# One layer of a diffusion transformer on one core: order inside the norm periods, the queue of the weights' loads, and where operands stand in SBUF

## The reference

```python
attn_in = _adaln(x, cond, ln1_w, ln1_b, g1_w, g1_b, b1_w, b1_b)
x = _attn(attn_in, attn_in, sa_wq, sa_wkv, sa_wo, sa_bo) + x
cross_in = _adaln(x, cond, ln1_w, ln1_b, g1_w, g1_b, b1_w, b1_b)
ctx_n = _ln(context, ca_lnc_w, ca_lnc_b)
x = _attn(cross_in, ctx_n, ca_wq, ca_wkv, ca_wo, ca_bo) + x
ffn_in = _adaln(x, cond, ln2_w, ln2_b, g2_w, g2_b, b2_w, b2_b)
h = gelu(ffn_in @ ff_w1 + ff_b1)
x = h @ ff_w2 + ff_b2 + x
# _attn: softmax(rope(q) @ rope(k).T / 8) @ v, then @ wo + bo
```

## The kernel before

| operand | before | with the change |
|---|---|---|
| xn_hi, xn_lo, ctx_hi, ctx_lo | 128 | 128 |
| w_hi, w_lo: weights of q and k | 192 | 192 |
| w_hi, w_lo: weights of v and of the output | 192 | 64 |
| o_hi, o_lo | 0 | 128 |
| hi (q, k) | 192, 0 | 0, 0 |
| lo (q, k) | 192, 0 | 192, 192 |
| pick, max_rows | 64, 192 | 192, 192 |
| hid_hi and hid_lo, w1, w2 | 0, 192, 192 | 0, 192, 192 |

## Time and profile before

### The profile page before, as it was taken

One profiled execution on the slowest core, in us unless ns is written; L12 is line 12 of the kernel. 1 busy time (PEld: TensorE's weight loads), 2 busy tenths in 40 slices (PEclk: granted clock), 3 DMA queues, 4 the chain that ended last, 5 costly groups with the idle time before them and its releaser, 6 DMA issues.

```text
span 1088.9 us, 18356 instructions
## 1 busy us (share of the span) xinstructions
PE 1071.9 (98%) x6908; PEld 758.4 (70%) x6908; DVE 854.3 (78%) x1017; ACT 640.5 (59%) x912; POOL 775.8 (71%) x502
## 2 busy tenths in 40 slices
PE   8899999999999999999999999999999999999998
PEld 6667766676667666776667766666677766666997
DVE  5887878778787787788888888888888888887555
ACT  6575565665666555566766555665555545786521
POOL 2688767787877876689999966887678767764210
PEclk8999999999999999999999999999999999999999
DMA  5322111311221111211122111221121111300001
GB/s 174 94 69 49 38 38 40 83 40 31 54 64 36 39 41 39 68 31 39 40 50 56 40 34 39 70 50 40 39 67 35 37 40 40 118 1 2 20 20 40
DMA packets 61096, 52.86 MB, mean 49 GB/s; under 512 B 23504, under 2 KB 43984, under 8 KB 60752
## 3 DMA queue, kind: packets, MB, share of 16 engines
q1 hardware_dynamic: 59232, 50.10, 19.4%
q10 hardware_dynamic: 1776, 1.59, 0.5%
HBM read 15.75 MB, written 2.10 MB: 16 GB/s over the span
## 4 chain that ended last, share of the span: by engine, by line
PE 91%; ACT 3%; DVE 2%; DMA 1%; issue 1%; POOL 1%; SPq 0%; ACTq 0%; POOLq 0%
PE ps L1029 18%; PE ps L813 9%; PE ps L814 8%; PE ps L815 8%; PE ps L966 6%; PE ps L888 6%; PE ps L1000 6%; PE ps L1014 6%; PE ps L972 5%; PE ps L970 5%; PE ps L968 5%; PE ps L1125 4%; PE ps L859 1%; PE ps L829 1%; PE ps L901 1%
## 5 line engine op out<-in xcount | busy, mean ns | idle before, releaser
L646 ACT ACTIVATE probs<-ps 128x1024 f32<-128x1024 f32 x256 | 262.4, 1026 | 198.7 <-PE ps L972 177.3
L1227 DVE TENSOR_REDUCE neg_max<-ps 128x2 f32<-128x1024 f32 x256 | 300.7, 1224 | 43.4 <-PE ps L1000 43.3
L503 POOL TENSOR_TENSOR acc<-acc,probs 128x1024 f32<-128x1024 f32 x126 | 301.2, 2391 | 18.1
L1029 PE MATMUL ps<-probs,v 128*64 128x512 f32 x1024 | 230.7, 592 | 0.0
L498 POOL TENSOR_TENSOR acc<-probs 128x1024 f32<-128x1024 f32 x64 | 152.3, 2380 | 43.6 <-ACT probs L646 43.6
L512 POOL TENSOR_TENSOR eo<-tmp 128x512 f32<-128x512 f32 x63 | 89.0, 1412 | 122.4 <-DVE tmp L1254 121.7
L1029 PEld LDWEIGHTS ps<-probs,v 128*64 128x64 f32 x1024 | 73.8, 137 | 145.5 <-issue 145.5
L1254 DVE TENSOR_TENSOR tmp<-ps,rope 128x1024 f32<-128x1024 f32 x126 | 148.4, 1213 | 16.2 <-PE ps L859 12.8
L1000 PE MATMUL ps<-hi 64*128 64x512 f32 x512 | 108.0, 410 | 3.3 <-issue 0.9
L966 PE MATMUL ps<-max_rows,pick 64*128 64x512 f32 x512 | 108.6, 412 | 1.9 <-DMA max_rows<-neg_max 1.5
L813 PE MATMUL ps<-xn_hi,w_hi 128*128 128x512 f32 x256 | 106.4, 416 | 1.4 <-DVE xn_lo L358 1.0
(11 more groups left out here) (134 smaller groups left out, 2184.7 us busy)
## 6 DMA issues: line engine op xcount, KB each, us to landing
lo<-eo SPq DMA_DIRECT2D x126, 256.0 KB, 3.3
w_raw<-pack_dram SPq DMA_DIRECT2D x16, 192.0 KB, 3.9
x<-x_dram SPq DMA_DIRECT2D x4, 512.0 KB, 7.9
w_raw<-pack_dram SPq DMA_DIRECT2D x8, 256.0 KB, 3.8
max_rows<-neg_max SPq DMA_DIRECT2D x128, 2.0 KB, 2.1
w_raw<-w_dram SPq DMA_DIRECT2D x2, 1024.0 KB, 5.4
out<-x SPq DMA_DIRECT2D x8, 256.0 KB, 2.2
ctx_in<-ctx_dram SPq DMA_DIRECT2D x4, 384.0 KB, 3.8
```

The source lines that it names most:

```text
L503: pool.tensor_tensor(acc[:, g % 2, :, :], acc[:, g % 2, :, :], probs[:, i, :, :], ALU.add).then_inc(added, 1)
L646: act.activation(probs[:, i, :, :], score_ps(i), ACT.Exp, scale=SCALE).then_inc(exped, 1)
L1029: mm = pe.matmul(av_ps(g)[DH * h:DH * h + DH, :], v[:, u % 2, kt, c:c + DH], probs[:, kt, h, :], start=(kt == 0), stop=(kt == TT - 1))
L1227: dve.tensor_reduce(neg_max[:, g % 2, :, i], peak_ps(i), AX.X, ALU.max, negate=True).then_inc(maxed, 1)
```

## The change

It has five parts.
- ACT: in the norm periods of the context `high_o(p-1)` stands ahead of `high_qk` and of the split of weights.
- The norm's variance plus epsilon: the addition (L1221, 16 times) goes from DVE to ACT, which does it with a bias of epsilon; the logarithm reads the variance itself. `STATS` and the counts of `ln_guess` follow.
- POOL: the biases of batches 1, 2 and 3 are added in periods 16, 21 and 23 rather than 15, 18 and 21.
- SP: `load_weights` stands between `land_max(p+1)` and `land(p+4)` rather than behind both.
- SBUF: the weights are two blocks with 32 elements between them, so that those of the values and of the output stand 128 bytes further on; q and k of `lo` and `hi` lose their offset to each other; gaps, `ones`, `pick` and `o_hi` move with them (the table above).

```diff
-        lo = asb("lo", [128, 2, 4 * N + 16], F32R)
-        gap("gap_hi", 32, attention_only)
-        hi = asb("hi", [128, 2, 2 * N + 16], F32R)
-        gap("gap_w", 32, attention_only)
-        w_hi = asb("w_hi", [128, 4, 2 * D], F32R)
-        w_lo = asb("w_lo", [128, 4, 2 * D], F32R)
+        lo = asb("lo", [128, 4, 2, N], F32R)
+        gap("gap_hi", 16)
+        hi = asb("hi", [128, 2, 2, N], F32R)
+        gap("gap_w", 48)
+        w_hi = asb("w_hi", [128, 2, 4 * D + 32], F32R)
+        w_lo = asb("w_lo", [128, 2, 4 * D + 32], F32R)
...
+        def w_of(tensor, m):
+            return tensor[:, m // 2, m % 2 * 2 * D:(m % 2 + 1) * 2 * D]
...
-        bias_in.update({13: 0, 15: 1, 18: 2, 21: 3})
+        bias_in.update({13: 0, 16: 1, 21: 2, 23: 3})
...
-        STATS = 2 * TT + 1
+        STATS = 2 * TT
...
             for p in range(PAIRS):
                 if is_pair(p + 1):
                     land_max(p + 1)
+                if p % 8 == 1 and p // 8 < NP - 1:
+                    w = p // 8
+                    sp.wait_ge(w_split, 4 * w + 3)
+                    load_weights(w + 1)
                 if is_job(p + 4):
                     land(p + 4)
...
             def guess_rstd(n):
                 act.wait_ge(ln_step, STATS * (n + 1))
-                act.activation(rstd[:, :], var_eps[:, :], ACT.Ln).then_inc(ln_guess, 1)
-                act.wait_ge(ln_guess, 2 * n + 1)
+                act.activation(var_eps[:, :], mean_var[:, :, 1], ACT.Identity, bias=eps[:, :]).then_inc(ln_guess, 1)
+                act.activation(rstd[:, :], mean_var[:, :, 1], ACT.Ln, bias=eps[:, :]).then_inc(ln_guess, 1)
+                act.wait_ge(ln_guess, 3 * n + 2)
                 act.activation(rstd[:, :], rstd[:, :], ACT.Exp, scale=-0.5).then_inc(ln_guess, 1)
...
+                rows_first = p in rows_in_period and order[rows_in_period[p]][0] == C
+                if rows_first:
+                    high_o(p - 1)
                 if is_pair(p + 2):
                     high_qk(p + 2)
                 if p in split_in:
                     split_weights(*split_in[p])
-                if is_pair(p - 1):
+                if is_pair(p - 1) and not rows_first:
                     high_o(p - 1)
...
-                dve.wait_ge(ln_step, STATS * n + 2 * TT)
-                dve.tensor_scalar(var_eps[:, :], mean_var[:, :, 1], EPS, None, ALU.add).then_inc(ln_step, 1)
```

More of the change, by code:

```diff
@@ L55, in build @@
         ident = sb("ident", [128, 128])
-        zero = sb("zero", [128, 1])
+        eps = sb("eps", [128, 1])
         cols = sb("cols", [128, 8 * KT + FT])
@@ L73, in asb, with gap @@
             return sb(name, shape, dt, attention_only)
-        def gap(name, size, where=stack):
+        def gap(name, size, where=attention_only):
             sb(name, [128, size], F32, where)
@@ L99, in build @@
         max_rows = asb("max_rows", [128, N], F32R)
[L100 removed]
         pick = asb("pick", [128, 128], F32R)
[L102 removed]
+        ones = asb("ones", [128, DH])
+        gap("gap_o", 48)
         o_hi = asb("o_hi", [128, 3, N], F32R)
         o_lo = asb("o_lo", [128, 3, N], F32R)
[L105 removed]
         av = asb("av", [128, N])
@@ L109, in build @@
         attention_only.close()
-        gap("gap_w1", 40)
+        gap("gap_w1", 40, stack)
         w1_hi = sb("w1_hi", [128, KT, FF], F32R)
@@ L117, in build @@
         w2_raw = sb("w2_raw", [128, FT, D])
-        gap("gap_hid", 16)
+        gap("gap_hid", 16, stack)
         hid_hi = sb("hid_hi", [128, 4, N], F32R)
@@ L126, in build @@
         raw_qk = lo.bitcast(F32)
-        def qk(tensor, slot):
-            return tensor[:, :, slot * N:(slot + 1) * N]
+        def w_of(tensor, m):
+            return tensor[:, m // 2, m % 2 * 2 * D:(m % 2 + 1) * 2 * D]
         def tmp_of(j):
@@ L365, in low_weights @@
                     c = slice(kt * D, (kt + 1) * D)
-                    split = eng.tensor_tensor(w_lo[:, m, c].rearrange("p (e a f) -> p e a f", e=2, a=4),
+                    split = eng.tensor_tensor(w_of(w_lo, m)[:, c].rearrange("p (e a f) -> p e a f", e=2, a=4),
                                               w_raw[:, m, c].rearrange("p (a e f) -> p e a f", e=2, a=4),
-                                              w_hi[:, m, c].rearrange("p (e a f) -> p e a f", e=2, a=4),
+                                              w_of(w_hi, m)[:, c].rearrange("p (e a f) -> p e a f", e=2, a=4),
                                               ALU.subtract)
@@ L454, in _ @@
                     load_ctx_ln()
-                if p % 8 == 1 and p // 8 < NP - 1:
-                    w = p // 8
-                    sp.wait_ge(w_split, 4 * w + 3)
-                    load_weights(w + 1)
                 if p % 8 == 3 and p // 8 < NP - 1:
@@ L481, in _ @@
         def _(pool):
+            pool.memset(eps[:, :], EPS).then_inc(const_ready, 1)
             pool.memset(ident[:, :], 0.0).then_inc(const_ready, 1)
-            pool.memset(zero[:, :], 0.0).then_inc(const_ready, 1)
             pool.memset(pick[:, :].bitcast(F32), 1.0).then_inc(const_ready, 1)
@@ L724, in period @@
                         split_ffw(0, c)
+            act.wait_ge(const_ready, 1)
             guess_rstd(0)
@@ L858, in project_rest @@
                         c = slice(256 + e * 128, 256 + (e + 1) * 128)
-                        mm = pe.matmul(job_ps(j, e), w_[half, 1, c], a_[half, b, 1, :], start=False, stop=(n == 2))
+                        mm = pe.matmul(job_ps(j, e), w_of(w_, 1)[half, c], a_[half, b, 1, :], start=False, stop=(n == 2))
                         if n == 2:
@@ L887, in project_v @@
                         for n, (a_, w_) in enumerate(((a_hi, w_hi), (a_hi, w_lo), (a_lo, w_hi))):
-                            mm = pe.matmul(v_ps(u, tt), a_[:, b, kt, cut], w_[:, 2, c],
+                            mm = pe.matmul(v_ps(u, tt), a_[:, b, kt, cut], w_of(w_, 2)[:, c],
                                            start=first and kt == 0 and n == 0, stop=(phase == 0 and kt == KT - 1 and n == 2),
@@ L900, in project_v_rest @@
                             cut = slice((2 * r + t) * 128, (2 * r + t + 1) * 128)
-                            mm = pe.matmul(v_ps(u, 2 * r + t), a_[half, b, 1, cut], w_[half, 2, 256:512],
+                            mm = pe.matmul(v_ps(u, 2 * r + t), a_[half, b, 1, cut], w_of(w_, 2)[half, 256:512],
                                            start=False, stop=(n == 2), skip_group_check=True)
@@ L962, in score @@
                 half = (slice(0, DH), slice(DH, 128))
-                q_hi, k_hi = qk(hi, g % 2)[:, 0, :], qk(hi, g % 2)[:, 1, :]
-                q_lo, k_lo = qk(lo, g % 4)[:, 0, :], qk(lo, g % 4)[:, 1, :]
+                q_hi, k_hi = hi[:, g % 2, 0, :], hi[:, g % 2, 1, :]
+                q_lo, k_lo = lo[:, g % 4, 0, :], lo[:, g % 4, 1, :]
                 for h in range(2):
@@ L999, in peak @@
                     half = slice(DH * h, DH * h + DH)
-                    mm = pe.matmul(out[:, h, :], qk(hi, g % 2)[half, 0, cut], qk(hi, g % 2)[half, 1, :], start=True, stop=True)
+                    mm = pe.matmul(out[:, h, :], hi[half, g % 2, 0, cut], hi[half, g % 2, 1, :], start=True, stop=True)
                 mm.then_inc(peaked, 1)
```

27 lines of the change are left out of this document (12 added, 15 removed).

## The result

| | before | with the change |
|---|---|---|
| median, us | 1093.06 (5 runs) | 1086.88 (5 runs) |
| lowest and highest | 1091.41, 1093.84 | 1085.21, 1088.16 |
| profiled execution | 1090.72 | 1087.08 |
| its span | 1088.9 | 1085.0 |

The ratio is 0.9941, with a 95% interval of 0.9929 to 0.9953: 6.4 us faster, between 5.1 and 7.8. The forecast was 7.5 us and 1085.3. It is right in sign and nearly in size, but three of its terms failed (epsilon, the loads and the values' weights), and one that it held at zero, the scores, made up for part of them. One run of the kernel before, beside the first experiments, took 3712.7 us in place of 1093; it enters no ratio.

The account below looks back on a forecast made before the run. PE, busy 98% of its span, was taken to bound the kernel. Terms 4.3 + 0.9 + 2.5 - 0.2 = 7.5 us off the 1092.8 median gave 1085.3 us, range 1082.5 to 1090.8.

Parts of the forecast that it names:

- the scores: PE's score steps under the new operand offsets: taken as zero, with 2 us kept on either side.
- Part 1, the orders: `high_o` ahead of `high_qk` in norm periods ends PE's waits: 4.3 us with the biases' help, from 2.7 to 4.8.
- the 0.5 left for periods 7 and 15: PE in periods 7 and 15: a wait of 0.05 and a slow step of 0.20 stay in each, 0.5 us together.
- Part 2, the biases: Bias on POOL out of period 18 ends its hold on DVE's `low_qk`: 0.7 us, counted in the orders' 4.3.
- 0.7 of the 0.82: Share of PE's 0.82 us wait in period 19 laid to period 18's bias on POOL slowing DVE's `low_qk`.
- Rival 3: Norm periods give back part: follow-on waits stay or `low_qk` of period 16 or 23 starts behind the bias; 1087.6 us, chance 0.14.
- Part 3, epsilon: Addition of epsilon off DVE shortens PE's waits at periods 32 and 62: 0.9 us, from 0.4 to 1.2.
- Part 4, the loads: Weights' loads moved on SP into its wait for POOL's rotation: zero gain, zero cost.
- Part 5, places: Values' matmuls on PE with the stationary operand 64 bytes past the moving one, 117.5 to 113.6 ns: 2.5 us gained.
- Rival 4: Score steps pay for q and k without their offset: 8 ns over 1024 steps, 8.2 us lost, 1095.8 us; chance 0.05.
- Rival 1: The offsets do nothing and something other than place slows L888: gain 5.2 us, 1087.6 us; chance 0.18.
- The 0.2 taken off in the sum: PE's steps from a projection to the output: 0.2 us of loss subtracted from the summed gain.

Follow-up runs that it names:

- e_order: The kernel before with only `high_o` ahead of `high_qk` and the biases at periods 16, 21 and 23; ratio to before 0.9960.
- e_high: The kernel before with only `high_o` ahead of `high_qk` in the four norm periods, biases as before; ratio to before 0.9974.
- m_pace: Separate kernel of matmuls of ones at 16 pairs of operand offsets, other engines idle, then DVE and POOL busy; 113.3 to 120.0 ns per 256-column matmul.
- e_loads_back: The changed kernel with the weights' loads back in their old place behind `land(p+4)`; ratio to before 0.9945.
- e_places: The kernel before with only the new places in SBUF, all orders as before; ratio to before 0.9992.
- f_late2: The changed kernel with DVE's `low_qk` of periods 2 and 32 behind the rotations and `add_out`; ratio to before 0.9933.
- e_eps: The kernel before with only the addition of epsilon moved from DVE to ACT; ratio to before 1.0005.
- m_entry: Separate kernel of matmuls of ones: runs of 24 entered from different groups, then DVE beside POOL copies; runs end at 113.2 to 113.4 or 117.6 to 117.9 ns.
- e_flat: The changed kernel with `o_hi`, `o_lo` and the output's weights at their old places; ratio to before 0.9936.

## Why the prediction was nearly right, and where it was not

**Part 1, the orders: right.** 4.3 predicted, 4.4 measured (e_order, interval 2.7 to 6.0), 4.5 in periods 6 to 19 of its trace. The cause on ACT, the slack of 0.6 and the follow-on waits held; the 0.5 left for periods 7 and 15 was mostly not needed (0.44 went to 0.24, the step behind it to 0.38).

**Part 2, the biases: the mechanism right, its size wrong.** The term "0.7 of the 0.82" took the collision as it stood. It moves with DVE: e_high shows that the wait would have grown to 1.56, so the bias's move carries 1.4 us of the 4.4. Rival 3's mechanism did not occur in periods 16 and 23, but by little: `low_qk` starts 0.4 and 0.2 us ahead of the bias there (295.61 against 296.02, 402.09 against 402.29), and it is POOL's bias that is held, 3.4 us in place of the 2.41 that the forecast gave it.

**Part 3, epsilon: wrong, 0.9 predicted, 0 measured.** Both local gains came as sized (0.36 and 0.44). The step that failed is "Without L1221 the first is gone", where I asked what is late next on PE, but not beside what DVE's earlier operation would now start. It is rival 3 at another place: the bias of period 32, which the change does not touch.

That the one that starts second is held shows in m_pace too: the two-operand subtraction (L61), alone 1.23, takes 3.2 to 3.3 in the 20 of its 24 turns in which POOL's addition (L44) was first, 2.95 on average (that addition takes 2.34 to 2.41 beside L63, and 3.44 in the one turn in which L61 was first, by 0.04), and with one operand in PSUM (L63) 1.22:

```profile
L44 POOL TENSOR_TENSOR pa<-pa 128x1024 f32<-128x1024 f32 x48 | 139.3, 2903 | 130.1 <-PE ps L90 126.4
L61 DVE TENSOR_TENSOR da<-da 128x1024 f32<-128x1024 f32 x24 | 70.7, 2945 | 115.5 <-PE ps L90 114.8
...
L63 DVE TENSOR_TENSOR da<-ps,da 128x1024 f32<-128x1024 f32 x24 | 29.4, 1224 | 0.8
```

**Part 4, the loads: wrong, 0 predicted, 0.9 us in the traces** of e_loads_back and of the change. "An issue would have to take 1 us for ten of them to make `land` late" looked at the item behind them in their new place. In their old place the item behind is `land_max` of the next period, and for it 0.8 us an issue is enough. "No wait of PE for a transfer of maxima stands in these periods" was true by less than 0.1 us.

**Part 5, places: wrong in its reason, mis-sized in both directions.** The step that failed is "what differs is the place of the operands", followed by a relation that sets the pace. (L888 and L1125 do both write 256 of the 512 columns of one of the eight parts of the kernel's `ps`.) The runs have two rhythms (113.3 and 117.8 ns); 64 past does not give the short one, it only makes it more frequent. The values' runs gained 0.8 us in the changed kernel in place of 2.5 (13 of 32 short; 1.2 to 1.5 in e_places, f_late2 and e_loads_back), the output's, held unchanged, lost 0.9 (20 in place of 30; 0.2 in e_places), and the scores, held at zero, gained about 2.0. The bound of 2 us either way for them was right. The 233.4 and 228.2 of the second table are the reason for 1.7 of it: two of the five steps gave up a stationary operand at 64 past for an equal one. The two steps at the peak, -0.8 and +0.6, are not explained. Rival 4 named the same term with the wrong sign: for the pairs equal offsets are the fastest, though for matmuls of 256 columns they are the slowest. It also counted four steps with a new relation where the table of operands has three (L966 to L968 keeps 64 past and L972 to L1000 equal offsets), 768 in place of 1024, so that its own price would have given 6.1 us and 1093.7. Rival 1, that the offsets do nothing, fell: m_pace reads 113.3 to 120.0 ns for one instruction by address and history. Yet its number, 1087.6, was nearer to 1086.9 than mine, and its gain of 5.2 as near to 6.4 as my 7.5, since the offsets' net gain was small for other reasons. The 0.2 taken off in the sum was an estimate for the steps from a projection to the output, and no run shows it: the step from the projection's last matmul to the output's first is 231 ns or less in 20 of 30 of before, and 235 to 236 in 13 of 30 of the changed kernel, so about 0.1 in all.

**The sum.** By runs of parts: 4.4 for the orders, -0.5 for epsilon, 0.9 for the places, makes 4.8; the whole is 6.4. (PE's busy time fell by 2.5 us, as the forecast's last sentence asked.) The 1.6 between are the loads and what they take from the other parts when they stay: against before, the first score steps of periods 35 and 43 lose 0.9 us in e_order, 0.4 in e_eps and 0.7 in e_places, 2.0 in all, and nothing in the changed kernel. Each figure of a total has an interval of 1.0 to 1.6 us to either side, so the split rests on these traces and not on the totals. That the forecast came within 1.1 us of the gain is in good part luck: 0.9 for epsilon and 1.7 of the values' 2.5 did not come, the output lost 0.9, and the scores' 2.0 and the loads' share, both held at zero, made up for most of it.

## What to carry to other kernels

Where an operation is taken off an engine, look at what the next ones will then start beside: a subtraction that starts 0.4 us behind another engine's addition in place of 0.3 ahead of it cost a full microsecond, and moved behind operations that read PSUM it took 1.22 there (f_late2, period 32) in place of 3.10. In periods 16, 21 and 23 of the changed kernel the same race is won by 0.2 to 0.4 us only. In a queue, count all items behind the ones that move, in their old place as in the new, and compare the landing with the step that needs it, since a wait of 0.07 us grows with each gain made elsewhere. Before a difference in pace is put down to addresses, list the paces of single runs, not their mean: two values and nothing between them point to a state, which a relation of the run's own addresses cannot explain. Where the count of such runs varies between kernels that hold the addresses, as from 13 to 22 here, one trace does not show what a placement is worth.

## What the hardware showed that was not expected

- Matmuls of 128 rows and 256 columns and operands 64 bytes apart run in one of two rhythms, 113.3 or 117.8 ns, held through runs of 24 (m_entry); at equal offsets 119.5 to 120.0 (m_pace). The group ahead probably chooses; what else does is open.
- Pairs of 64 rows over 512 columns with contiguous operands follow the offsets in m_pace: 228.2 equal, 229.5 with the stationary operand 64 before, 232.4 at 128 apart, 233.4 at 64 past.
- A copy on POOL also holds DVE's two-operand subtraction, for 1.94 us in place of 1.23 (m_entry, five of six), and POOL's additions hold DVE's copy of one SBUF operand, for up to 2.8 us in m_pace, where it takes 0.69 when POOL is done.
- The granted clock is at half of full for some stretches in the first 65 us, not the same in every execution: it reads 0.50 from 10 to 15 us in before, and from 11 to 14 and from 42 to 45 in the changed kernel. The changed kernel and then before, in the first two stretches of 27 us (the third figure from the right is the clock):

```profile
0.00:27.00 27.00, 21.25 (x104) 17.46 (x104) 15.22 (x43) 17.20 (x34) 7.74 (x20) 0.94 0.60 175
27.00:54.00 27.00, 24.36 (x126) 17.15 (x128) 21.41 (x40) 14.19 (x23) 18.70 (x17) 0.94 0.36 95
```

```profile
0.00:27.00 27.00, 22.00 (x104) 18.36 (x104) 15.34 (x45) 16.42 (x32) 7.72 (x20) 0.87 0.58 173
27.00:54.00 27.00, 23.90 (x132) 16.48 (x132) 23.74 (x43) 13.96 (x23) 18.50 (x17) 1.00 0.37 97
```

Steps of 0.23 take 0.43 in such a stretch (L972 to L974 at 42.72 in the changed kernel). Among 22 runs of before beside the first experiments, 11 with a mean clock of 0.997 or more have a mean of 1092.3 us, 11 with 0.994 or less 1094.1. And the wait in period 3 goes with it: of the traced kernels with `low_qk` in its old order, all that had half clock in period 0 with a wait gone in period 1 have the wait in period 3 (from 0.8 us in e_flat to 1.3 in e_loads_back, with the slow step behind it), and the others have none. e_order has it too, though its edits touch no period before 6, so that wait is not of the change, and the runs behind one median may have it or not.
